# Layer 0 of a four-layer kernel: first tiles ahead of the rank factors, factor loads on ScalarE's queue, high planes two pieces late, transpositions one block behind the norms

## The reference

```python
x = x + _layernorm(_L0_attn_ref(_layernorm(x), Wq, bq, Wk, bk, Wv, bv))
x = x + _layernorm(_L0_ffn_ref(_layernorm(x), gate_w, gate_su, gate_sv, up_w, ...))

def _anemll_linear(x, w, su, sv):
    w_eff = w * (su @ sv)            # su @ sv has rank 4
    return jnp.einsum('bsh,oh->bso', x, w_eff)
# ffn: down( silu(gate(x)) * up(x) ), hidden size 1792 = 14 blocks of 128
```

## Time and profile before

| what | us |
|---|---|
| median of 3 runs | 4204.03 |
| lowest, highest run | 4203.64, 4207.63 |
| the profiled execution | 4209.37 |
| its span | 4207.6 |
| PE, DVE, ACT, POOL busy in the span | 3712.3, 2792.1, 2269.8, 1909.4 |
| first gate matmul of group 0 | 85.81 |
| first down matmul of group 0 | 192.48 |

### The profile page before, as it was taken

One profiled execution on the slowest core, in us unless ns is written; L12 is line 12 of the kernel. 1 busy time (PEld: TensorE's weight loads), 2 busy tenths in 40 slices (PEclk: granted clock), 3 DMA queues, 4 the chain that ended last, 5 costly groups with the idle time before them and its releaser, 6 DMA issues.

```text
span 4207.6 us, 62985 instructions
## 1 busy us (share of the span) xinstructions
PE 3712.3 (88%) x21602; PEld 1850.4 (44%) x21602; DVE 2792.1 (66%) x4493; ACT 2269.8 (54%) x3911; POOL 1909.4 (45%) x1578
## 2 busy tenths in 40 slices
PE   3889998889888779999999999999999975867899
PEld 2344443223322345555555555555555542443344
DVE  4444345664675468888888888988888866566322
ACT  4533224455455466667666666766676644453222
POOL 4600000000000348787777878777777774463000
PEclk9999987899888899999999999999999997898999
DMA  3200011001100100000000000000000010012000
GB/s 104 63 6 1 1 31 16 1 2 26 27 7 4 40 12 1 25 13 25 13 20 18 4 25 10 25 13 20 18 7 24 1 49 15 23 46 76 29 10 20
DMA packets 62919, 91.62 MB, mean 22 GB/s; under 512 B 12406, under 2 KB 36489, under 8 KB 62597
## 3 DMA queue, kind: packets, MB, share of 16 engines
q1 hardware_dynamic: 61928, 86.94, 7.2%
q10 hardware_dynamic: 672, 0.59, 0.1%
HBM read 73.85 MB, written 6.85 MB: 19 GB/s over the span
## 4 chain that ended last, share of the span: by engine, by line
PE 62%; DVE 14%; issue 8%; ACT 6%; POOL 3%; DMA 1%; DVEq 0%; ACTq 0%; POOLq 0%; SPq 0%
PE psum L329 13%; PE psum L331 13%; PE psum L330 13%; PE psum L1563 3%; DVE arena L1725 3%; PE psum L1536 2%; PE psum L2670 2%; PE psum L2658 2%; PE psum L2666 2%; PE psum L2627 2%; PE psum L1547 2%; DVE x L2352 1%; PE psum L2649 1%; PE psum L1532 1%; ACT xn L218 1%
## 5 line engine op out<-in xcount | busy, mean ns | idle before, releaser
L329 PE MATMUL psum<-xt_hi,arena 128*128 128x512 f16 (+2 forms) x2272 | 875.0, 385 | 31.1 <-DVE arena L588 9.1
L330 PE MATMUL psum<-xt_lo,arena 128*128 128x512 f16 (+2 forms) x2272 | 873.4, 384 | 0.0
L331 PE MATMUL psum<-xt_hi,arena 128*128 128x512 f16 (+2 forms) x2272 | 872.9, 384 | 0.0
L2453 POOL TENSOR_TENSOR arena<-arena 128x1024 f16<-128x1024 f16 x256 | 515.4, 2033 | 49.5 <-DVE arena L2264 32.3
L329 PE MATMUL psum<-arena 128*128 128x512 f16 (+1 forms) x1152 | 421.8, 370 | 61.2 <-DVE arena L3081 19.6
L1725 DVE TENSOR_REDUCE arena<-psum 128x1 f32<-128x512 f32 (+3 forms) x608 | 366.4, 655 | 162.8 <-PE psum L1536 161.8
L1676 ACT ACTIVATE arena<-psum 128x512 f32<-128x512 f32 x576 | 320.1, 598 | 285.0 <-PE psum L1547 187.4
L331 PE MATMUL psum<-arena 128*128 128x512 f16 (+1 forms) x1152 | 421.9, 370 | 0.0
L330 PE MATMUL psum<-arena 128*128 128x512 f16 (+1 forms) x1152 | 421.9, 370 | 0.0
L1481 POOL TENSOR_TENSOR rs<-sd,epsc 128x1 f32<-128x1 f32 x15 | 8.1, 540 | 830.0 <-DVE sd L1773 830.0
L329 PEld LDWEIGHTS psum<-xt_hi,arena 128*128 128x128 f16 (+1 forms) x2272 | 224.8, 99 | 279.8 <-issue 17.3
(11 more groups left out here) (354 smaller groups left out, 7532.5 us busy)
## 6 DMA issues: line engine op xcount, KB each, us to landing
arena<-m_wi SPq DMA_DIRECT2D x64, 320.0 KB, 2.9
arena<-m_wo SPq DMA_DIRECT2D x32, 256.0 KB, 2.6
arena<-arena SPq DMA_DIRECT2D x90, 64.0 KB, 2.6
x<-L_attn_x SPq DMA_DIRECT2D x4, 1024.0 KB, 5.2
out<-x SPq DMA_DIRECT2D x4, 1024.0 KB, 4.4
arena<-gate_wT SPq DMA_DIRECT2D x16, 224.0 KB, 2.5
arena<-up_wT SPq DMA_DIRECT2D x16, 224.0 KB, 2.5
arena<-down_wT SPq DMA_DIRECT2D x14, 256.0 KB, 2.6
```

Source lines behind the costliest of these rows:

```text
L329: nc.tensor.matmul(out, lh, rh, start=start, stop=False)
L330: nc.tensor.matmul(out, lh, rl, start=False, stop=False)
L331: return nc.tensor.matmul(out, ll, rh, start=False, stop=stop)
L2453: nc.gpsimd.tensor_tensor(m4_ar[:, q], heads[q].broadcast_to([P, HG, P]), m4_le.unsqueeze(1).broadcast_to([P, HG, P]), ALU.mult).then_inc( ...
```

## The change

Four things are done, all in layer 0.

1. The statistics and norms of the first four tiles come ahead of the step `factors` (the two VectorE instructions that make the factors' low planes). The 18 small factor loads go from SyncE's queue to ScalarE's; ScalarE waits for VectorE's memset and for GpSimd's six constants, one of which is now the memset of `fac_n`. SyncE issues the attention's weights and the second quarter of x ahead of all weight pieces. The summing of Wq gets a step of its own (`w0`).
2. In the step `chunk` of piece n, ScalarE casts and GpSimd subtracts for piece n-2 (before: n-1), and there are four raw buffers in place of three.
3. Ahead of group 0's first block stand 14 `chunk` steps (before: 16), and the entries 8 to 11 use both PSUM banks.
4. In the groups' blocks a `tr` stands behind the `up` of its block (before: between gate and up), and `hi`, `lo` and the norm after next one block later. Batches start at block 0 (x0) and block 7 (ln) in place of 2 and 8.

```diff
-        RAW1 = 3
+        RAW1 = 4
...
         def bank0(n):
-            return 6 + n % 2 if n < 2 * GT else 6
+            return 6 + n % 2 if n < 3 * GT else 6
...
             def chunk(n=1):
...
-                    if made <= len(chunks):
+                    if made < len(chunks) + 2:
...
-            steps.append(("factors", 0))
-            steps += [("stat", n + j) for j in range(GT)] + [("var", n)]
-            chunk(2)
-            steps += [("scale", n), ("norm", n), ("norm", n + 1)]
+            steps += [("stat", n + j) for j in range(GT)] + [("var", n), ("scale", n), ("norm", n), ("norm", n + 1), ("factors", 0)]
             for j in range(GT):
                 steps += planes(n + j)
                 if j + 2 < GT:
                     steps.append(("norm", n + j + 2))
+                if j == 0:
+                    steps.append(("w0", 0))
+                elif j < 3:
+                    steps.append(("stat", m + j - 1))
                 chunk()
...
                 def batch(n, f):
-                    add(after, f, *[("stat", n + j) for j in range(GT)], ("var", n))
-                    add(after, f + 1, ("scale", n), ("norm", n), ("norm", n + 1))
+                    add(f, *[("stat", n + j) for j in range(GT)], ("var", n))
+                    add(f + 1, ("scale", n), ("norm", n), ("norm", n + 1))
                     for j in range(GT):
-                        add(before, f + 2 + j, ("tr", n + j))
-                        add(after, f + 2 + j, ("hi", n + j), ("lo", n + j))
+                        add(f + 2 + j, ("tr", n + j))
+                        add(f + 3 + j, ("hi", n + j), ("lo", n + j))
                         if j + 2 < GT:
-                            add(after, f + 2 + j, ("norm", n + j + 2))
+                            add(f + 3 + j, ("norm", n + j + 2))
+                if g + 2 < NG:
+                    batch(entry0("x0", (g + 2) * GT), 0)
                 if g + 1 < NG:
...
-                    batch(entry0("ln", (g + 1) * GT), 8)
-                if g + 2 < NG:
-                    batch(entry0("x0", (g + 2) * GT), 2)
+                    for q, part in enumerate(ATTN0):
+                        add(1 + q, (part, g + 1))
+                    batch(entry0("ln", (g + 1) * GT), 7)
...
+            sp_l0_attn(sp)
+            load_x(sp, 1)
             for i, (m, k, cols, _, _) in enumerate(chunks):
-                if i == 2:
-                    sp_l0_attn(sp)
-                if i in (4, 10, 16):
-                    load_x(sp, 1 + (i - 4) // 6)
+                if i in (12, 20):
+                    load_x(sp, 2 + (i - 12) // 8)
...
         def pool_consts(pool, ch):
+            nc.gpsimd.memset(fac_n[0:FR], 0.0).then_inc(consts_ok, 1)
...
-                    if n:
-                        m, k, cols, h_, l_ = chunks[n - 1]
+                    if n >= 2:
+                        m, k, cols, h_, l_ = chunks[n - 2]
                         w = cols.stop - cols.start
-                        pool.wait_ge(w1_hi, n)
-                        nc.gpsimd.tensor_tensor(l_, raw1[:, (n - 1) % RAW1, 0:w], h_, ALU.subtract).then_inc(w1_lo, 1)
+                        pool.wait_ge(w1_hi, n - 1)
+                        nc.gpsimd.tensor_tensor(l_, raw1[:, (n - 2) % RAW1, 0:w], h_, ALU.subtract).then_inc(w1_lo, 1)
...
         def act_l0(act):
-            act.wait_ge(consts_ok, 5)
+            act.wait_ge(w1_made, 1)
+            act.wait_ge(consts_ok, 6)
+            for m, (wide, narrow) in enumerate((("gate_suT", "gate_sv"), ("up_suT", "up_sv"), ("down_sv", "down_suT"))):
+                for part in range(3):
+                    rows = slice(32 * part + RANK * m, 32 * part + RANK * (m + 1))
+                    act.dma_start(fac_w[rows, :], A[wide]).then_inc(w1_fac, 16)
+                    act.dma_start(fac_n[rows, m, :], A[narrow]).then_inc(w1_fac, 16)
```

More of the change, by code:

```diff
@@ L434, in steps0 @@
                     steps.append(("norm", n + j + 2))
+                if j == 0:
+                    steps.append(("w0", 0))
+                elif j < 3:
+                    steps.append(("stat", m + j - 1))
                 chunk()
-            m = entry0("x0", GT)
             steps.append(("qkv", 0))
-            steps += [("stat", m), ("stat", m + 1)]
-            chunk(2)
[L440 to L445, removed]
+            chunk()
+            steps += [("logits", 0), ("stat", m + 2), ("stat", m + 3), ("var", m)]
+            chunk()
+            steps += [("maxima", 0), ("scale", m), ("norm", m), ("norm", m + 1)]
+            chunk()
+            steps += [("weights", 0), *planes(m), ("norm", m + 2)]
+            chunk()
+            steps += [("means", 0), *planes(m + 1), ("norm", m + 3), ("add", 0)]
+            chunk(2)
             n = entry0("ln", 0)
@@ L448, in steps0 @@
             chunk()
-            steps += [("norm", m + 3), *planes(m + 2), *planes(m + 3), ("scale", n), ("norm", n), ("norm", n + 1)]
+            steps += [*planes(m + 2), *planes(m + 3), ("scale", n), ("norm", n), ("norm", n + 1)]
+            chunk()
             for j in range(GT):
@@ L456, in steps0 @@
             for g in range(NG):
[L457 to L458 removed]
+                after = {}
+                add = lambda f, *what: after.setdefault(f, []).extend(what)
                 def batch(n, f):
[L461 to L462 removed]
+                    add(f, *[("stat", n + j) for j in range(GT)], ("var", n))
+                    add(f + 1, ("scale", n), ("norm", n), ("norm", n + 1))
                     for j in range(GT):
[L464 to L465 removed]
+                        add(f + 2 + j, ("tr", n + j))
+                        add(f + 3 + j, ("hi", n + j), ("lo", n + j))
                         if j + 2 < GT:
[L467 removed]
+                            add(f + 3 + j, ("norm", n + j + 2))
+                if g + 2 < NG:
+                    batch(entry0("x0", (g + 2) * GT), 0)
                 if g + 1 < NG:
[L469 to L474 removed]
+                    for q, part in enumerate(ATTN0):
+                        add(1 + q, (part, g + 1))
+                    batch(entry0("ln", (g + 1) * GT), 7)
                 for f in range(F0):
@@ L1125, in pool_l0 @@
         def pool_l0(pool):
+            pool.wait_ge(consts_ok, 6)
             for what, n, *f in STEPS0:
@@ L1231, in act_l0 @@
         def act_l0(act):
-            act.wait_ge(consts_ok, 5)
-            for what, n, *f in STEPS0:
-                if what == "factors":
-                    act.wait_ge(w1_fac, 18 * 16)
-                    nc.scalar.activation(fac_wh[0:FR, :], fac_w[0:FR, :], ACT.Copy, scale=WS).then_inc(w1_made, 1)
-                    nc.scalar.activation(fac_nh[0:FR], fac_n[0:FR], ACT.Copy, scale=WS).then_inc(w1_made, 1)
-                elif what == "norm":
+            act.wait_ge(w1_made, 1)
[5 more added lines that the diff above has]
+                    act.dma_start(fac_n[rows, m, :], A[narrow]).then_inc(w1_fac, 16)
+            act.wait_ge(w1_fac, 18 * 16)
+            nc.scalar.activation(fac_wh[0:FR, :], fac_w[0:FR, :], ACT.Copy, scale=WS).then_inc(w1_made, 1)
+            nc.scalar.activation(fac_nh[0:FR], fac_n[0:FR], ACT.Copy, scale=WS).then_inc(w1_made, 1)
+            for what, n, *f in STEPS0:
+                if what == "norm":
                     b, j = BATCH0.index(n // GT * GT) % 2, n % GT
@@ L1253, in act_l0 @@
                 elif what == "logits":
-                    act.wait_ge(a0_lg, n + 2)
-                    nc.scalar.activation(lg0, lg0, ACT.Exp, scale=float(D0) ** -0.5).then_inc(a0_ex, 1)
+                    act.wait_ge(a0_lg, 2 * n + 2)
+                    nc.scalar.activation(lg0, lg0, ACT.Exp, scale=float(D0) ** -0.5).then_inc(a0_lg, 1)
                 elif what == "chunk":
@@ L1335, in dve_l0 @@
                                             xt_hi[:, :, ds(i * P, P)], ALU.subtract).then_inc(xt_ok, 1)
-                    if n == 0:
-                        dve.wait_ge(a0_in, 96)
-                        nc.vector.tensor_reduce(w0[:, :, 0:D0], w0q, AXX, ALU.add).then_inc(a0_w, 1)
-                        nc.vector.tensor_reduce(b0[:, 0:D0], b0q, AXX, ALU.add).then_inc(a0_w, 1)
-                        nc.vector.memset(sc0, 0.0).then_inc(a0_lg, 1)
+                elif what == "w0":
+                    dve.wait_ge(a0_in, 96)
+                    nc.vector.tensor_reduce(w0[:, :, 0:D0], w0q, AXX, ALU.add).then_inc(a0_w, 1)
+                    nc.vector.tensor_reduce(b0[:, 0:D0], b0q, AXX, ALU.add).then_inc(a0_w, 1)
+                    nc.vector.memset(sc0, 0.0).then_inc(a0_lg, 1)
                 elif what == "qkv":
```

33 lines of the change are left out of this document (12 added, 21 removed).

## The result

The changed kernel takes 4236.02 us (median of 7 runs, 4221.44 to 4245.25), the kernel before, on the same chip, 4203.64 (7 runs): a ratio of 1.0078, 95% interval 1.0066 to 1.0091. It is slower, by 32.4 us; the forecast of 4219.8 had the sign and half of the size. The profiled execution took 4236.02 with a span of 4234.2, 26.6 more than that of before.

What follows compares the result with a forecast made beforehand. TensorE, busy 88% of the span, was taken as the bound. Front -17.6, groups 0 to 2 +14.3, +2.7 and +6.15, clock +10.2 sum to +15.8 us: 4219.8 on the median of 4204.0, range 4196 to 4234.

Steps and rivals of the forecast that it cites:

- The turns: Blocks of groups 0 to 2: transpositions wait for `lo` behind the product, 2.25 us idle in group 0, 2.05 in group 2.
- Rival B: Blocks: VectorE makes `lo` before the turn needs it, turns cost at most 0.5 us, 4185; chance 0.12 with its soft form.
- The clock: Layer 0's blocks: 13 half clock spells after idles against 7 before, +10.2 us, between 0 and +20.
- rival D: Layer 0's blocks: every idle brings a half clock spell, +10 us more, 4230; chance 0.16.
- The front: Before group 0's blocks: factors land at 14.0 us, projection at 30.0, first gate at 68.2, -17.6 us.
- Rival C: Front: factor loads land at the bulk's end, at 23 us, +8.6 us more, 4228; chance 0.10.
- The second piece of lag: Front: casting for the piece two back removes VectorE's 4.0 us wait for a high plane.
- Group 0's waits: Group 0's blocks and down entry: TensorE idle 30.0 us against 15.7, +14.3 us.
- Block 10: Group 0: the 32nd low plane comes 6.6 us after block 9, GpSimd having stopped for a power; 5.9 us idle.
- The down entry: Group 0's down stage: two more `chunk` steps behind the last block, 8.1 us idle, bounds 5 and 9.
- the turns with the copy ahead of entry 13: Group 0's blocks: entry 13 idles 4.8 us, entries 14 and 15 4.5, entries 17 to 19 6.75.

Runs made afterwards that it cites:

- Experiments 3: The changed kernel with both PSUM banks alternating for all entries' turns, not only the first 12: 4179.22 against 4199.46, ratio 0.9946.
- experiment 4: The changed kernel, still one bank, with `hi` and `lo` between gate and up, ahead of VectorE's product: 4188.32 against 4199.46, ratio 0.9970.
- experiment 1: The changed kernel with the block loop of before; new front and late planes stay: 4210.99 against 4199.46, ratio 1.0021.
- experiment 6: The changed kernel with the product's low plane moved behind `lo` in blocks that hold a `lo`: 4220.48 against 4204.88, ratio 1.0039.
- experiment 5: The changed kernel with SyncE's bulk loads held until the 18 factor loads have landed: 4235.17 against 4204.88, ratio 1.0069.
- experiment 7: The changed kernel with planes one piece late again and three raw buffers: 4240.82 against 4204.88, ratio 1.0078.
- experiment 8: The changed kernel with both banks for all entries and three more weight pieces ahead of the first gate: 4179.84 against 4204.88, ratio 0.9933.

## Why the prediction was half right

**The turns: right.** The idles in front of transpositions, their releaser, and their sizes came as worked out from VectorE's order: 2.08 us in group 2 for 2.05, 2.21 and 2.37 in group 0 for 2.25. Group 1 had 14.9 us for 13.55: three of its turns were set down at 1.9 and took 2.07 or 2.08 like those of group 2, and the other three took 3.22 and twice 2.71 for 2.75 and twice 2.55. Experiments 3 and 4 show the mechanism from two sides. Rival B, `lo` ahead of the product, names the very edit of experiment 4; its condition was not met in the change, and where the edit made it so, the kernel was faster (4188.32).

**The clock: the step that failed, 8 us of the 16 missing.** The term of +10.2 us for spells of half clock measured +18.0. It rests on this sentence: "By nearest row, idles of 2.25 us count as 2.37 (a spell), idles of 1.9 as 1.88 (none)." I compared the idle from product to `lo` (1.9) with a row's 1.88, though I had just worked out 2.05 with the handoff to the transposition, and that is what stands in brackets in such a row. It lies between two rows, 1.88 without a spell and 2.37 with one, and I took the nearer as if there were a sharp edge. Of the six turns of groups 1 and 2 that waited 2.07 or 2.08 us, for which I had counted no spell, five had one; at 1.7 us each that is 8.5 us. Two of the five stand in group 2 (6.2 us idle, 3.9 more busy). Over layer 0 of all twelve profiles, from the first gate matmul on, 20 of 27 idles of 2.0 to 2.15 us in front of a turn had a spell, 26 of 29 of 2.15 to 2.45, and none of 11 between 1.4 and 1.9 (a spell is counted where the granted clock of the next 3.4 us is below 0.9; it was 0.71 or less in all of them). Longer idles go free now and then, too: 2.46 us in experiment 4 and 2.79 in experiment 1. So what came is rival D, except for the idles that go free. By the Trainium skill (TensorE: Matmul & The Clock Gate, "A second HAM failure mode: psum-queue depth-cycling"), cycling through PSUM banks leaves micro-idles between matmul groups that make the clock oscillate. The windows at 0.63 and 0.59 behind 2.08 us agree; experiment 6's 1.47 us at 1.00 show a length that is let through.

**The front: the second step that failed, 6.2 us too much.** It gained 11.4 us for 17.6. The factors landed at 19.42 instead of 14.0. My bounds were 12.8 and 23; experiment 5 shows that the bulk makes the difference (12.6 without it). The table load ran at 10.01 while the factors flew, where I had placed it behind them, which gave back 1.3. So the low planes were done at 24.57 + 1.75 = 26.3 and not 22.2, and the projection came at 34.57 and not at 30.0. The way from there to the gate took 39.9 us for 38.2; the add in it took 5.0 where the earlier trace rows had 4.3. Rival C, at 23, was nearer than my value. The second piece of lag, to which I gave 4.0 us, had no part in it (experiment 7). The Trainium skill's rule of the prediction (DMA: Bandwidth & Descriptors, "Queues, rings and completion order") says that each DMA engine goes round robin between the queues. The trace agrees: the loads took 9.9 us, and still landed ahead of x's second quarter, which SyncE had issued at 7.16 and which took until 22.0. But the rule told nothing about how much the factors would lose.

**Group 0's waits: right.** Block 10 cost 6.2 us for 5.9, in two idles: 1.79 ahead of a rank product behind block 9 and 4.40 ahead of the gate. GpSimd made the power from 147.08 on, then four pieces, and the 32nd low plane at 157.38, 7.1 us behind block 9 where I had 6.6. The down entry cost 7.7 us in four idles (0.47, 1.62, 0.40, 5.18) for 8.1, the turns with the copy ahead of entry 13 16.4 for 16.05. Sum: 30.3 for 30.0.

**The range.** It ended at 4234, 2 us short. C and D each stood alone in the list, at 4228 and 4230. They don't exclude each other and both came for the most part (6.2 us of C's 8.6, 7.8 of D's 10); together they would have been 4238 (8.6 and 10 on the forecast's 4219.8).

What stays open: what sets how long the rest of the program, with the same matmuls, runs at the lower clock (3605 to 3634 us in different profiles), and so why experiment 8's total didn't follow its layer 0; and what decides which of two equal idles gets its spell. A measurement with the layers' start shifted by known amounts was not made.

## What to carry to other kernels

Before placing a step "as early as possible", look what stands ahead of its release on the releasing engine: a turn that waits for an instruction queued behind the product of the block just issued costs TensorE the whole tail of that block, each time. In dense matmul work count an idle of 2 us or more as its length plus, in most cases (46 of 56 here between 2.0 and 2.45 us), half of a half clock spell's 3.4 us, and try to get it below 1.5 or away; a second buffer, or the two steps in another order, did both here. A shortened front leaves less time for the engine that makes the weights beside it, so give that engine its pieces ahead in the same edit. And rivals that can come true together belong in the range as their sum.

## What the runs showed of the hardware

**The clock answers idles of about 2 us, mostly.** In full matmul work 1.47 us idle left the granted clock at 1.00 each time; 2.08 us was followed by about 0.6 in two of three cases of one group, with the same blocks ahead of each.

**Small loads beside a bulk.** 18 factor loads on ScalarE's queue, 0.3 MB, were complete 9.9 us behind the last issue with the bulk on SyncE's queue in flight, and 3.5 us behind it (issued at 9.15, complete at 12.63) when SyncE held the bulk back in experiment 5. Wq took 9.3 us to land in the changed kernel and 5.5 in experiment 5.

**A table load ran ahead of a wait.** It stood at 13.65 behind the wait for the loads when SyncE had issued them, and at 10.01 directly behind ScalarE's last issue, 9.4 us before its ACTIVATE, in the changed kernel; in experiment 5 it ran at 9.51 and the ACTIVATE at 12.63. Why the two placements differ no run shows.

**VectorE beside GpSimd.** The same four adds of 128x512, in the kernel before without GpSimd's work beside them:

```profile
283.68 2.50 DVE L1384 TENSOR_TENSOR x<-x,arena 128x512 f32<-128x512 f32 x4
```

and in experiment 8 with GpSimd making planes:

```profile
55.55 5.95 DVE L1385 TENSOR_TENSOR x<-x,arena 128x512 f32<-128x512 f32 x4
```

They took 2.50, 4.27, 5.00 (changed kernel) and 5.95 us. GpSimd had no instruction beside the first four, two beside the second, three beside the third and five beside the last. The Trainium skill (SBUF — State Buffer, "Who interferes with whom") has a port pair that both engines take as an exclusive lock. The rows agree as far as VectorE takes longer while GpSimd works, and give the price; that one stands still for the other they do not show.
